# Expert stage with rows turned two steps ahead and five places for weighed rows: a change in the order of an attention and mixture-of-experts kernel

## The reference: what is computed

```
y = layernorm(x)
y = layernorm(y + causal self attention(y))
y = layernorm(y + cross attention(y, context of 1601 rows))
y = layernorm(y + relu(y w1 + b1) w2 + b2);   x1 = x + y
h = layernorm(x1);  logits = h wg';  the best 2 of 8 experts, their weights normed to 1
out = x1 + sum over the 2 experts of weight * w2[e] (silu(w1[e] h) * w3[e] h)
```

## Time and profile before

| | us |
|---|---|
| median of 3 runs | 526.02 |
| lowest, highest | 524.81, 528.18 |
| the profiled execution, its own time | 526.67 |
| its span, first to last instruction | 524.2 |
| PE busy | 496.8 (95%) |
| DVE busy | 378.8 (72%) |
| ACT busy | 286.7 (55%) |
| POOL busy | 278.0 (53%) |

### The profile page before, as it was taken

How to read it: one execution, slowest core, us unless ns; L and a number is a source line. 1 busy time by engine, 2 the same in 40 slices (tenths; PEclk the granted TensorE clock), 3 DMA queues, 4 the chain that set the end, 5 groups by cost and what they waited for, 6 DMA issues and landing times.

```text
span 524.2 us, 10993 instructions
## 1 busy us (share of the span) xinstructions
PE 496.8 (95%) x3686; PEld 326.6 (62%) x3686; DVE 378.8 (72%) x978; ACT 286.7 (55%) x575; POOL 278.0 (53%) x312
## 2 busy tenths in 40 slices
PE   7899999999999999999999999999999899999970
PEld 3576766656666676766667776656666566666650
DVE  5899887588967668877889899997878444444440
ACT  4556767647466745773749657664454344433320
POOL 4463203003642708994496763545754756757573
PEclk9999999999999999999999999999999999999995
DMA  8002533246877537985598770248597689778683
GB/s 273 19 25 77 171 102 108 94 96 105 149 175 121 148 74 168 156 147 167 98 191 178 158 264 20 90 111 114 110 194 110 113 131 122 137 117 139 102 93 38
DMA packets 135313, 65.60 MB, mean 125 GB/s; under 512 B 109757, under 2 KB 126590, under 8 KB 135262
## 3 DMA queue, kind: packets, MB, share of 16 engines
q1 hardware_dynamic: 127774, 54.69, 48.6%
q0 software_dynamic: 7488, 10.23, 12.2%
HBM read 28.19 MB, written 10.35 MB: 74 GB/s over the span
## 4 chain that ended last, share of the span: by engine, by line
PE 58%; DVE 11%; DMA 8%; issue 8%; ACT 6%; POOL 4%; POOLq 2%; SPq 1%; DVEq 0%; ACTq 0%
PE ps L1205 47%; DMA out<-y,qst 5%; DMA probT<-prob 3%; PE ps L1300 3%; PE ps L1302 3%; PE ps L1301 3%; ACT ps L1016 2%; DVE cmax L1744 2%; POOL out L968 2%; POOLq L962 1%; POOL y L942 1%; ACT tT L1002 1%; ACT prob L1015 1%; PE ps L1214 1%; PE ps L1261 1%
## 5 line engine op out<-in xcount | busy, mean ns | idle before, releaser
L1205 PE MATMUL ps<-arena,probT 128*128 128x256 f16 (+2 forms) x1092 | 180.0, 318 | 4.0 <-issue 1.8
L1205 PEld LDWEIGHTS ps<-arena,probT 128*128 128x128 f16 (+1 forms) x1092 | 104.4, 97 | 61.0 <-issue 8.3
L1205 PE MATMUL ps<-arena,qT 128*128 128x512 f16 (+1 forms) x384 | 69.1, 332 | 1.0 <-DVE prob L1885 0.7
L968 POOL DMA_INDIRECT out<-y,qst x39 | 62.9, 1612 | 13.1 <-issue 7.8
L1015 ACT ACTIVATE prob<-ps,nbias 128x512 f16<-128x512 f32 x64 | 39.0, 609 | 50.9 <-DVE nbias L1750 50.9
L1143 ACT ACTIVATE w1m<-ps 128x512 f32<-128x512 f32 x39 | 23.3, 598 | 74.7 <-PE ps L1205 56.6
L1205 PE MATMUL ps<-arena,tT 128*128 x468 | 57.4, 273 | 0.9 <-DVE tT L2445 0.6
L791 POOL TENSOR_TENSOR rstd<-veps,expo 128x1 f32<-128x1 f32 x16 | 9.0, 563 | 91.8 <-DVE veps L1779 91.8
L1205 PEld LDWEIGHTS ps<-arena,qT 128*128 128x128 f16 x384 | 32.5, 97 | 36.0 <-issue 1.7
L942 POOL DMA_INDIRECT y<-hrow,qst x39 | 40.4, 1037 | 24.1 <-DVE qst L2107 12.8
L1205 PE MATMUL ps<-tT 128*128 128x512 f16 (+3 forms) x234 | 48.8, 346 | 1.4 <-DVE probT L1810 0.8
(11 more groups left out here) (240 smaller groups left out, 919.5 us busy)
## 6 DMA issues: line engine op xcount, KB each, us to landing
stage<-we_in SPq DMA_DIRECT2D x33, 256.0 KB, 3.0
prob<-we_in SPq DMA_DIRECT2D x15, 256.0 KB, 3.8
xin<-x_in SPq DMA_DIRECT2D x16, 128.0 KB, 2.7
out<-y SPq DMA_DIRECT2D x16, 128.0 KB
hrow<-tT SPq DMA_DIRECT2D x4, 512.0 KB, 3.5
y<-x_in SPq DMA_DIRECT2D x3, 512.0 KB, 7.6
stage<-z_in SPq DMA_DIRECT2D x4, 256.0 KB, 5.7
prob<-w_in SPq DMA_DIRECT2D x4, 256.0 KB, 3.2
```

The source lines that it names most:

```text
L968: g.indirect_dma_start(out[:rows_of(p), :], bass.IndirectOffsetOnAxis(ridx[:, n:n + 1], 0), ys[:, n % RING, :], None, compute_op=ALU.add). ...
L1205: r = t.matmul(o, lhs(a), rhs(b), start=first and n == 0, stop=last and n == 2)
```

## The change

Seven edits:

- `ys` gets five places in place of four (`YR`). Semaphores, the table's constants and the waits of `weighted` and `add` count by fives. `s_norm` and `s_affine` of the last block go behind: DVE does it at the end of step 2, POOL a tile later.
- PE turns the rows of tile n + 2 in step n, not n + 1 (`turn_tiles`). The first tile of each later phase (9 and 17) stays one step ahead, so two tiles are turned in steps 8 and 16. Since turned rows then share a PSUM bank with the routing products of the same step, PE waits there for ACT's copy.
- In `add` the register is loaded ahead of all waits.
- A table `before2` gives the count for n - 2 where the ring turns over (tiles 11, 16, 21, 26, 31, 36), so no tile but 6 waits for n - 2 blindly within a phase. These tiles load two registers.
- The `gap` instruction is gone. Its wait becomes a wait of the sequencer; the addition itself carries the wait for addition n - 3.
- Two gathers (6 and 7) stand ahead of a norm and of the gates of the third block.
- At the start of the experts two copies on ACT change places, and so do splits of weights and gated products on DVE.

```diff
-                wait(pool, "x1_out", 16 * TB * PHASES[p][0])
-                alone = n <= RING or n == PHASES[p][1]
+                alone = n <= YR or n == PHASES[p][1]
+                if not alone:
+                    if n == PHASES[p][1] + 1 or n == YR + 1:
+                        wait(pool, "r_next", p + 1)
+                    done = pool.value_load(before[0:1, n:n + 1], min_val=16, max_val=16 * NJ)
+                    if n % YR == 1 and n > YR + 1:
+                        done2 = pool.value_load(before2[0:1, n:n + 1], min_val=16, max_val=16 * NJ)
                 if n > 2:
                     add_done(n - 3)
-                if n > 1 and (alone or n % RING == 1):
+                if n > 1 and (alone or n == YR + 1):
                     add_done(n - 2)
                 if n and alone:
                     add_done(n - 1)
                 if not alone:
-                    if n == PHASES[p][1] + 1 or n == RING + 1:
-                        wait(pool, "r_next", p + 1)
-                    done = pool.value_load(before[0:1, n:n + 1], min_val=16, max_val=16 * NJ)
-                    pool.wait_ge(sm[f"e_add{(n - 1) % RING}"], done)
-                    if n % RING != 1:
-                        pool.wait_ge(sm[f"e_add{(n - 2) % RING}"], done)
-                    g.tensor_tensor(gap[:, n:n + 1], expo[:, 0:1], expo[:, 0:1], ALU.mult)
+                    pool.wait_ge(sm[f"e_add{(n - 1) % YR}"], done)
+                    if n % YR != 1:
+                        pool.wait_ge(sm[f"e_add{(n - 2) % YR}"], done)
+                    elif n > YR + 1:
+                        pool.wait_ge(sm[f"e_add{(n - 2) % YR}"], done2)
+                wait(pool, "x1_out", 16 * TB * PHASES[p][0])
                 wait(pool, "e_y", n + 1)
...
+        def turn_tiles(n):
+
+            late = [PHASES[p][1] for p in (1, 2)]
+            return [k for k in range(RING, NJ) if n == (k - 1 if k in late else k - 2)]
...
-                if i == 1:
+                if i == 2:
                     s_affine(NB - 1)
...
+            gather(5)
+            gather(6)
+            gather(7)
             rstd_of("n_", NB - 1)
-            gather(5)
             gates(2)
             weigh(2)
-            issued = 6
+            issued = 8
...
-                if nxt:
-                    x_trans(n + 1, (s + 1) % RING)
+                for k in turn_tiles(n):
+                    x_trans(k, k % RING)
...
+                if n in (H_AT, LOGITS_AT, RANKS_AT) or n in LISTS_AT:
+                    wait(pe, "e_xcp", n + 3)
...
-                if i == 2:
-                    s_norm(NB - 1)
                 between(early[1:], own)
...
+                if i == 2:
+                    s_norm(NB - 1)
...
+                m0 = max(n0, 1)
+                v.scalar_tensor_tensor(before2[:, m0 + 1:n1], differ[:, m0 + 1:n1], 16.0, adds[:, m0 - 1:n1 - 2],
+                                       ALU.mult, ALU.add)
...
-                dve.wait_ge(sm[f"e_add{s}"], 4 * (n - s))
-                v.tensor_scalar(ys[:, s, :], psO[s % 2][:, :D], rgate[:, n:n + 1], None,
+                wait(dve, f"e_add{n % YR}", 16 * (n // YR))
+                v.tensor_scalar(ys[:, n % YR, :], psO[s % 2][:, :D], rgate[:, n:n + 1], None,
                                 ALU.mult).then_inc(sm["e_y"], 1)
```

More of the change, by code:

```diff
@@ L70 @@
 RING, AHEAD, BEHIND = 4, 8, 3
+YR = 5
 LEAD = 2
@@ L102, in xattn_ffn_moe @@
         bridge = sb("bridge", [P, 3])
-        gap = sb("gap", [P, NJ])
+        before2 = sb("before2", [P, NJ], U32)
         iota8 = sb("iota8", [P, NE])
@@ L168, in xattn_ffn_moe @@
         sil = w1m[:, 0:2 * NI].rearrange("p (q c) -> p q c", q=2)
-        ys = y[:, RING:2 * RING, :]
+        ys = y[:, RING:RING + YR, :]
         qst = sb("qst", [P, 2, D])
@@ L325, in xattn_ffn_moe @@
             e_x0 e_x1 e_x2 e_x3 e_a0 e_a1 e_a2 e_a3 e_xtr e_xcp e_up e_sil e_act e_ahi e_alo e_down e_y
-            e_add0 e_add1 e_add2 e_add3 e_ltr e_lcp""".split()
+            e_add0 e_add1 e_add2 e_add3 e_add4 e_ltr e_lcp""".split()
         sm = {n: sem(n) for n in names}
@@ L721, in _ @@
                     store_h(sp, NB - 1)
-            for s in range(RING):
-                wait(sp, f"e_add{s}", 16 * len(range(s, NJ, RING)))
+            for s in range(YR):
+                wait(sp, f"e_add{s}", 16 * len(range(s, NJ, YR)))
         @block.gpsimd
@@ L775, in _ @@
             iota(jot[:], [[1, NJ]])
-            iota(adds[:], [[16, (NJ + 1) // RING], [0, RING]])
+            iota(adds[:], [[16, (NJ + 1) // YR], [0, YR]])
             iota(iotaP[:], [[1, P]])
@@ L945, in add_done @@
             def add_done(n):
-                wait(pool, f"e_add{n % RING}", 16 * (n // RING + 1))
+                wait(pool, f"e_add{n % YR}", 16 * (n // YR + 1))
             def add(n):
                 p = phase_of(n)
-                wait(pool, "x1_out", 16 * TB * PHASES[p][0])
-                alone = n <= RING or n == PHASES[p][1]
+                alone = n <= YR or n == PHASES[p][1]
[5 more added lines that the diff above has]
+                        done2 = pool.value_load(before2[0:1, n:n + 1], min_val=16, max_val=16 * NJ)
                 if n > 2:
                     add_done(n - 3)
-                if n > 1 and (alone or n % RING == 1):
+                if n > 1 and (alone or n == YR + 1):
                     add_done(n - 2)
@@ L1149, in act_hi, with e_step @@
                 copy(arow[:, s, 0, :], ps[2 * (s % 2) + 1][:]).then_inc(sm["e_ahi"], 1)
-            def e_step(n, s, nxt=True):
+            def e_step(n, s):
                 silu(n, s % 2)
-                if nxt:
-                    x_copy(n + 1, 1 - s % 2)
+                for k in turn_tiles(n):
+                    x_copy(k, k % 2)
                 act_hi(n, s)
@@ L1161, in weighted @@
                 wait(act_, "r_list", [p for p in range(3) if n >= PHASES[p][1]][-1] + 1)
-                if n < RING:
-                    wait(act_, "x1_out", 16 * TB * (NB - 2))
-                else:
-                    act_.wait_ge(sm[f"e_add{s}"], 4 * (n - s))
-                a.activation(ys[:, s, :], psO[s % 2][:, :D], ACT.Copy, scale=rgate[:, n:n + 1]).then_inc(sm["e_y"], 1)
+                if n < YR:
+                    wait(act_, "x1_out", 16 * TB * (NB - 2 if n < RING else NB - 1))
+                else:
+                    wait(act_, f"e_add{n % YR}", 16 * (n // YR))
+                a.activation(ys[:, n % YR, :], psO[s % 2][:, :D], ACT.Copy, scale=rgate[:, n:n + 1]).then_inc(sm["e_y"], 1)
             x_copy(0, 0)
@@ L1177, in _ @@
             act_hi(1, 1)
+            h_copy(2, 1)
             x_copy(3, 1)
-            h_copy(2, 1)
             for n in range(2, E_LOOP):
                 silu(n, n % 2)
-                if n > 2:
-                    x_copy(n + 1, 1 - n % 2)
+                for k in turn_tiles(n):
+                    x_copy(k, k % 2)
                 if n == H_AT - 1:
@@ L1191, in _ @@
             for n in range(E_LOOP, NJ):
-                e_step(n, n % RING, n + 1 < NJ)
+                e_step(n, n % RING)
             wait(act_, "e_ltr", 1)
@@ L1614, in e_step @@
                     h_trans(NB - 1, 1)
+                if n == H_AT + 2:
                     wait(pe, "h_cp", 3)
-                if n == LOGITS_AT + 1:
+                if n == LOGITS_AT + 2:
                     wait(pe, "r_lg", NB)
-                if n == RANKS_AT + 1:
+                if n == RANKS_AT + 2:
                     routing_read(NB - 1)
-                if n - 1 in LISTS_AT:
-                    wait(pe, "r_list", LISTS_AT[n - 1] + 1)
-                if nxt:
-                    x_trans(n + 1, (s + 1) % RING)
+                if n - 2 in LISTS_AT:
+                    wait(pe, "r_list", LISTS_AT[n - 2] + 1)
+                for k in turn_tiles(n):
+                    x_trans(k, k % RING)
                 if n == BEHIND + 1:
@@ L1646, in _ @@
             for n in range(2, E_LOOP):
-                e_step(n, n % RING, n > 2)
+                e_step(n, n % RING)
             for n in range(E_LOOP, NJ - 1):
@@ L2365, in _ @@
             act_lo(0, 0)
+            gated(1, 1)
             rest_lo(dve, 10)
-            rest_lo(dve, 11)
-            gated(1, 1)
+            act_lo(1, 1)
             for m in range(TB):
                 out_stats(j, m)
-            act_lo(1, 1)
             out_moments(j)
+            rest_lo(dve, 11)
             rest_lo(dve, 12)
```

4 lines of the change are left out of this document (2 added, 2 removed).

## The result

| | before | changed |
|---|---|---|
| median, us (19 runs each, same chip) | 527.12 | 529.92 |
| ratio, 95% interval | | 1.0062 (1.0047 to 1.0077) |
| profiled execution, its own time | 526.67 | 531.75 |
| its span | 524.2 | 530.0 |
| last addition issued | 515.96 | 521.77 |

By the ratio the change costs 3.3 us (0.62% of 527); the medians lie 2.8 apart. The two profiled executions lie 5.1 apart, and that of the changed kernel is 1.8 above its median, so the pair by itself overstates the loss.

What follows compares the result with a forecast made beforehand. POOL's chain of additions, running behind PE, was taken to bound the end. Chain +2.2, self norm -0.5, turning two ahead -0.4, late gathers +0.6 gave +1.9 us: 527.9 us against the median of 526.02, range 521.0 to 531.0.

Steps and rivals of the forecast that it cites:

- the largest term: Twelve waits for a landed addition on POOL's chain: each dearer without `gap`, +4.9 us in all.
- the two early terms: Effects ahead of the last chain: self norm moved behind, -0.5 us; turning two ahead, -0.4 and +0.6 us.
- The gap instruction: POOL's chain of additions: without `gap`, landing to next issue costs 0.41 to 0.47 us more at twelve links, +4.9 us.
- the 0.54 us: Stretch ahead of an addition without `gap`, nothing shown awaited; read as preparation that `gap` lets the sequencer do meanwhile.
- The first rival: POOL's chain: a link costs the same without `gap`, sum -3.0 us, 523.0 us; chance 0.27.
- No `gap` at tiles that don't wait: POOL's additions that await no landing: -0.8 us behind gathers and -0.3 us behind additions, seven tiles each.
- tile 37: Near the chain's end: no blind wait for addition 35 any more, follows in 1.90 us, not 3.48: -1.6 us.
- Turning two ahead: Expert stage on PE: -0.4 us at the entry, +0.6 us for late gathers at tiles 14 and 16.
- The gain of 0.4 at the entry: Entry of the expert stage: PE's 0.53 us wait at 360.91 and some tenths go; -0.4, as DVE is busier.
- Self norm: Near 144 us: PE's 1.03 us wait goes, 0.54 us of DVE work moves to the next tile; -0.5 us.
- Five places: Ring `ys`: DVE's waits for a place hardly reach PE, so 0; gives cover when the chain is later.
- The third rival: Expert stage: late gathers behind later additions make PE the bound, time 533 us; chance 0.08.

Runs made afterwards that it cites:

- e1: Changed kernel with the small POOL instruction back ahead of the addition, carrying the wait for addition n - 1: 524.01 us, ratio 0.9989.
- e2: Kernel before without the `gap` instruction, the addition's own wait now the one for the stores of x1: 532.26 us, ratio 1.0124.
- e9: Kernel before with five places, registers loaded ahead and the second table, and without the small POOL instruction: 526.05 us, ratio 1.0035.
- e3: Changed kernel with rows turned one step ahead again, the rest as changed: 526.67 us, ratio 1.0041.
- e6: Changed kernel with the gather of tile 11 ahead of the last block's norm, not behind it: 527.06 us, ratio 1.0056.
- e10: Changed kernel with the small POOL instruction back and the gather of tile 11 ahead of the norm, rows still turned two ahead: 521.85 us, ratio 0.9962.
- e5: Changed kernel with the last block's self norm in the middle of step 2 again, its scaling a step earlier: 528.03 us, ratio 1.0065.

## Why the prediction held, and where it didn't

The forecast was +1.9 us (0.36%), the runs show +3.3 (0.62%). In the profiled pair the ledger gives +0.44 up to the first gather, +1.25 to addition 9, +4.50 landing to issue, +2.25 flights, -2.63 rest, together the 5.81 between the last additions. Without the flights it is 3.6, close to what the runs say. So the direction came from the largest term. Against that 3.6 the forecast is 1.7 short: the two early terms were 2.0 too low (1.25 + 0.44 against -0.3), the links 0.4 too high, the rest 0.1 too low. The bounds of my terms, added up as they are written, give 526.0 to 531.4 and not the 525.5 to 530.8 of the sum.

- **The gap instruction, +4.9: right, a little high.** I took 0.41 more per link; it is 0.33 to 0.37, 4.3 us for the twelve. With tiles 10 and 17, which I had left out, the ledger has 4.5. e1 takes it away and e2 and e9 put it into the other kernel. That the 0.54 us is preparation of the addition which the sequencer does only behind its waits was my reading of the earlier trace rows. The sequencer's rows bear it out. In the changed kernel it stands at the next tile's register load 0.52 us behind the landing (511.75 to 512.27, above), and the addition is all that lies between in program order. In e1, around the landing at 503.81, the chain of waits has

```profile
503.13 0.71 issue
503.84 0.23 POOLq L963
```

L963 is the next tile's load there, 0.03 us behind the landing: the sequencer had passed the addition while the small instruction still waited. What it does in that time the traces don't show. The Trainium skill (DMA: Bandwidth & Descriptors, "Anatomy of one DMA — SWDGE (gpsimd) path") has some 50 ns for the dispatch. The traces have 0.49 us (changed) and 0.54 us (e2) in the place where it would stand; whether all of that is dispatch is not shown.
- **The first rival (0.27), a link costs the same:** it did not come, at 0.33 to 0.37 more per link. The waits for n - 1 and n - 2 are still the sequencer's; an addition that carries the wait for n - 1 itself wasn't tried and stays open.
- **No `gap` at tiles that don't wait, -1.1, and tile 37, -1.6: right.** Together -2.7, measured -2.6 (40.11 to 37.48).
- **Turning two ahead, +0.2 (-0.4 and +0.6): this step failed.** It costs 1.25 us (1.21 back in e3, 1.33 in e6). I looked for gathers that would come late at tiles 14 and 16 and passed over tile 11, whose gather stands behind the norm of the last block. The rows were there to be read: gather 11 at 375.45, the turn of tile 10 at 376.68. A turn at that place wants rows 1.23 us after their gather is issued, and none lands so soon: the shortest gather of every experiment took 2.7 or 2.8 us. At tile 14 PE did not wait: its turn came 3.53 us behind the gather (389.37 to 392.90), and gathers take 3.0 to 3.7 us in the median of each experiment, less than the additions by which I had priced them (3.9). At tile 16 it waited 0.47 us, as much as it had at 401.84 before for another reason. The gain of 0.4 at the entry didn't show in the distance of e10 (78.95) against before (78.74), and its reason was misread: DVE is not the busier engine there. In the kernel before PE is busy 31.9 of 33 us and DVE 28.3:

```profile
340.00:357.00 17.00, 16.44 (x143) 9.59 (x142) 14.78 (x54) 10.65 (x19) 8.02 (x11) 1.00 0.57 114
357.00:373.00 16.00, 15.47 (x125) 9.64 (x124) 13.56 (x40) 6.75 (x14) 8.08 (x7) 1.00 0.68 108
```

- **Self norm, -0.5: failed, with a sign that rests on two pairs (e5).** The push I had worked out (0.54 us of DVE work on to the next tile) was real, and PE paid it at 149 us. The wait it should have removed hung mainly on something else, since with the norm gone it only fell from some 0.9 to 0.8 on average. What else it hangs on is open.
- **Five places, 0: right with the small instruction, wrong without it.** With it they are worth only tile 37, which I had counted apart. Without it they save 4.7 us (0.9%, e2 against e9). My sentence that they "give cover when the chain is 3 us later" named this, but not its size.
- **The third rival (0.08), late gathers that make PE the bound:** the waits ahead of turns came (3.5 us of PE's busy time from 412 to 500), and were covered by the 7 us that PE has behind it, as its condition said.
- **What the changed profile should show:** 0.83 at the links (0.78), additions 1.9 apart (1.86), the wait of 1.03 near 144 gone (0.80), PE idle ahead of the turns of tiles 14, 16 and 32 (none, 0.47 and 0.68), last product near 509 to 512 (514.8, some 3 later than I said), last addition near 518 (521.77, in an execution with 2.25 us of longer flights).

## What to carry to other kernels

Where a queue's next transfer must wait for the last one to land, let a small instruction of the same engine carry that wait if the transfer is issued by an engine's sequencer behind it: here it was worth 0.33 to 0.37 us per link and 0.6 to 1.2% of the whole, though it looks like an instruction that does nothing. When work is moved a step earlier, check every tile's input against its new due time, above all where its transfer stands behind another engine's result in an in-order queue. And when a chain becomes slower, look at how many buffers tie the bound engine to it.

## What the runs showed of the chip that was not expected

- **Additions land later where a DMA turn is issued beside them.** In the twelve profiles, additions 9 to 36, the flight goes with when SP issues its turn of the halves. With no turn issued from 4 us before the addition to 5 us after: 3.79 us on average (43 additions, longest 4.28; all of tiles 33 to 36, where no gathers run either). With the nearest within half a us of it: 4.54 (66 additions, longest 6.13). With the nearest some 1 us ahead 4.09 (93), 1 us behind 4.49 (55, longest 6.26), 2 us off on either side 4.00 and 4.08 (38 and 37). The gather beside the addition is not what does it: of the 66, 11 have no gather within 2.5 us and average 4.52. With no turn within 1.5 us, additions up to tile 32 average 4.05 with a gather beside them (63) and 4.00 without (11). The chain has 14 flights in it, so 0.1 us in the mean flight is 1.4 us of the whole, more than most edits here. No run moved a turn on purpose.
- **A register load can take more than twice its usual time.** At tile 31 of the changed kernel, which loads two registers, the additions are 2.16 us apart, at tile 36, which does too, 1.86, as everywhere; I had 0, at most 0.5, for each. It is not the second load as such: at tile 31 the changed kernel and e5 (2.14 apart) have a first load of 0.66 and 0.71 us, and e3, e6 and e9, with 0.47, 0.30 and 0.30, stay at 1.86 to 1.90. Why the load is sometimes slow is open.
